# Two-layer decoder on one core: smaller groups in the quantised feed-forward, splits on other engines and in another order, and the last stage's base products started in the stage before

## The reference

```python
x = _layernorm(x + _L0_attn_ref(x, ...))       # a state-space mixer (hydra)
x = _layernorm(x + _L0_xattn_ref(x, ctx, ...)) # cross-attention, 16 heads of 96, 4 of k and v
x = _layernorm(x + _L0_ffn_ref(x, ...))        # quantised feed-forward, inner width 1792
x = _layernorm(x + _L1_attn_ref(x, ...))       # self-attention, 32 heads of 16, ALiBi
x = _layernorm(x + _L1_xattn_ref(x, ctx, ...)) # cross-attention, 32 heads of 128, 8 of k and v, rms norms
x = _layernorm(x + _L1_ffn_ref(x, ...))        # linear with routed LoRA

def _L0_ffn_ref(...):
    # dequantize(w, s, z) = (w - z) * s, with a row of z and s for every 128 rows of w
    gate = silu(x @ gate_proj)
    up = x @ up_proj
    return (gate * up) @ down_proj

def _L1_ffn_ref(...):
    q = x[:, 107:-1, :].mean(axis=1)
    routing = softmax(q @ router_W.T + router_b)
    base = x @ W.T + b
    t = einsum('bsd,erd->bser', x, A)
    return base + einsum('bser,eor,be->bso', t, B, routing) * 2
```

## Time and profile before

| | us |
|---|---|
| median of 3 runs | 1679.01 (1676.1 to 1681.4) |
| the profiled execution, its own time | 1680.96 |
| its span, first to last instruction | 1679.2 |
| PE busy | 1575.3 (94%) |
| DVE busy | 932.6 (56%) |
| ACT busy | 803.6 (48%) |
| POOL busy | 769.3 (46%) |
| mean granted clock of TensorE | 0.982 |

### The profile page before, as it was taken

The page is one execution under the profiler, slowest core; times in us unless marked ns, Lnnn a source line. Parts: engine busy times, 40 slices in busy tenths (PEclk is TensorE's granted clock), DMA queues, the critical chain, the costliest instruction groups (busy, mean ns, idle before and its releaser), DMA issues. The chain is left out here.

```text
span 1679.2 us, 29888 instructions
## 1 busy us (share of the span) xinstructions
PE 1575.3 (94%) x11188; PEld 1316.2 (78%) x11188; DVE 932.6 (56%) x1647; ACT 803.6 (48%) x2447; POOL 769.3 (46%) x625
## 2 busy tenths in 40 slices
PE   6999999999997699998999879999999999999978
PEld 3777897888886488878777678888888888888866
DVE  3847503333365778775667734555555555555755
ACT  3342325444443355536999724454454454544520
POOL 3403214343421788842533545555555545554423
PEclk9999999999999799999999999999999999999999
DMA  6100200010102552203000031101101101100001
GB/s 207 38 1 1 57 20 20 20 41 2 52 2 82 182 175 98 79 1 120 1 2 26 29 113 38 39 26 38 46 19 51 38 27 39 32 26 14 1 1 51
DMA packets 62258, 77.85 MB, mean 46 GB/s; under 512 B 12136, under 2 KB 41316, under 8 KB 62116
## 3 DMA queue, kind: packets, MB, share of 16 engines
q1 hardware_dynamic: 61652, 74.63, 13.9%
q0 software_dynamic: 464, 1.32, 0.3%
HBM read 73.85 MB, written 2.10 MB: 45 GB/s over the span
## 5 line engine op out<-in xcount | busy, mean ns | idle before, releaser
L1145 POOL TENSOR_TENSOR xa_rs<-xa_ms,minus_half 128x5 f32<-128x5 f32 x64 | 74.7, 1168 | 170.0 <-DVE xa_ms L1395 169.9
L1151 POOL TENSOR_TENSOR xa_prob<-xa_prob,xa_inv 128x512 f32<-128x512 f32 x64 | 66.7, 1042 | 136.2 <-DVE xa_inv L1362 136.2
L763 POOL TENSOR_TENSOR xa_prob<-xa_prob,xa_inv 128x1024 f32<-128x1024 f32 x32 | 60.7, 1896 | 140.8 <-DVE xa_inv L1023 140.8
L1342 ACT ACTIVATE xa_prob<-xa_prob,xa_peak 128x128 f32<-128x128 f32 x256 | 99.7, 391 | 41.9 <-DVE xa_peak L1406 41.9
L1390 DVE TENSOR_REDUCE xa_ssq<-pre 128x4 f32<-128x512 f32 x64 | 43.9, 686 | 135.6 <-ACT pre L1328 135.6
L1699 DVE SCALAR_TENSOR_TENSOR ff_acc<-ff_ring,ff_sT,ff_acc 128x512 f32<-128x512 f32 x140 | 100.4, 747 | 21.6 <-ACT ff_acc L1653 12.7
L1599 PE MATMUL ff_ring<-xT_hi,ff_w 128*128 128x512 f32 x224 | 91.7, 410 | 18.1 <-DVE ff_acc L1699 13.5
L100 PE MATMUL xa_qp<-late_q_hi,xT_hi 128*128 128x512 f32 x256 | 107.2, 419 | 0.0
L1328 ACT ACTIVATE pre<-xa_qp 128x512 f32<-128x512 f32 x64 | 38.2, 597 | 142.6 <-PE xa_qp L102 142.6
L100 PE MATMUL xa_rows<-late_o_hi,xa_out_hi 128*128 128x512 f32 x256 | 102.6, 401 | 1.9 <-DVE xtok L1369 1.9
L2092 ACT ACTIVATE pre<-pre,sa_peak 128x128 f32<-128x128 f32 x256 | 99.2, 397 | 9.5 <-DVE sa_peak L2131 9.3
(11 more groups left out here) (415 smaller groups left out, 5054.6 us busy)
## 6 DMA issues: line engine op xcount, KB each, us to landing
pre<-in_wq SPq DMA_DIRECT2D x8, 1024.0 KB, 5.8
late_raw_o<-in_wo SPq DMA_DIRECT2D x8, 1024.0 KB, 5.2
ff_dn_q<-in_down_w SPq DMA_DIRECT2D x7, 512.0 KB, 3.8
ff_dn_z<-in_down_z SPq DMA_DIRECT2D x7, 512.0 KB, 4.9
ff_dn_s<-in_down_s SPq DMA_DIRECT2D x7, 512.0 KB, 6.1
pre<-in_wq SPq DMA_DIRECT2D x16, 192.0 KB, 3.5
pre<-in_wo SPq DMA_DIRECT2D x16, 192.0 KB, 3.9
pre<-in_xT SPq DMA_DIRECT2D x2, 1024.0 KB, 13.7
```

The costliest lines, as they stand in the source:

```text
L763: pool.tensor_tensor(prob[:, t % 3, :, :], prob[:, t % 3, :, :], bc(inv[:, t % 3, :], 2, [P, Q, KEYS]), ALU.mult).then_inc(s["norm"], 1)
L1145: pool.tensor_tensor(rs[:, :], ms[:, :], m.minus_half[:, 0:Q + 1], ALU.pow).then_inc(s["rs"], 1)
L1151: pool.tensor_tensor(prob[:, u % 2, :, :], prob[:, u % 2, :, :], bc(inv[:, u % 2, :], 2, [P, Q, S]), ALU.mult).then_inc(s["norm"], 1)
L1342: last = act.activation(prob[:, u % 2, h, :], prob[:, u % 2, h, :], ACT.Exp, bias=peak[:, u % 2, h:h + 1], accum_out=total[:, u % 2, h:h + 1])
```

## The change

Six parts. (1) cross0's v weights are copied and subtracted in four pieces, PE waits for each in its first batch, and the fillers ahead go from 9 to 4. (2) ffn0's groups are made of one, two, two, one and one turns instead of two, two, two and one: rows are now 40 of 2 or 4 tiles. Rows, weights and down weights have new units; PE starts with the first piece of weights, fillers go from 7 to 2, and SP issues the gate and up loads of turn T + 1 ahead of `dn(T)`. (3) self's output weights are split on DVE. (4) cross1's first kv weights are split in two halves, with fewer fillers; in steps 0 to 7 POOL's splits have another order; the 20 fillers of step 2 are gone. (5) The banks of `qp`, `kvp`, `qt` and `score` are shared with lora, and `base(0)` to `base(3)` of lora are issued in cross1's tail, three in place of fillers. (6) lora begins with a low rank, has five row banks, and its last scale goes to ACT, for which DVE computes a shift. The core of the diff:

```diff
-                act.activation(v_hi, raw_v, ACT.Copy).then_inc(s["v_hi"], 1)
+                for c in range(KC):
+                    act.activation(v_hi[:, c, :], raw_v[:, c, :], ACT.Copy).then_inc(s["v_hi"], 1)
...
-                dve.wait_ge(s["v_hi"], 1)
-                dve.tensor_tensor(v_lo, raw_v, raw(v_hi), ALU.subtract).then_inc(s["v_lo"], 1)
+                for c in range(KC):
+                    dve.wait_ge(s["v_hi"], c + 1)
+                    dve.tensor_tensor(v_lo[:, c, :], raw_v[:, c, :], raw(v_hi[:, c, :]), ALU.subtract).then_inc(s["v_lo"], 1)
...
                     if t < 2:
                         roots(t)
-                        split_o(0, 2 * t)
-                        split_o(0, 2 * t + 1)
-                    if g <= G:
+                        split_o(0, t)
+                    if t == 2:
+                        split_o(0, 2)
+                        split_o(0, 3)
+                    if t == 3:
+                        split_kv(1, 0)
+                        split_kv(1, 1)
+                    if 4 <= t < B:
+                        split_q(1, b - 4)
+                        split_o(1, b - 4)
+                    if 1 < g <= G:
...
-                idle_products(pe, m, rows[:, 0:P], 5)
+                idle_products(pe, m, rows[:, 0:P], 2)
                 for t in range(UNITS):
                     project_kv(t)
                     if t == 2:
-                        idle_products(pe, m, rows[:, 0:P], 20)
+                        idle_products(pe, m, rows[:, 0:P], 0)
...
+                def base(b, read, n):
+                    pe.wait_ge(s["split_q"], PIECES_Q * G)
+                    pe.wait_ge(n4["lo"], b + 1)
+                    pe.wait_ge(s[read], n)
+                    for c in range(KC):
+                        three(pe, m.late.bank[b][:, :], m.xT_hi[:, c, b * P:(b + 1) * P], m.xT_lo[:, c, b * P:(b + 1) * P],
+                              q_hi[:, 0, c, :], q_lo[:, 0, c, :], c == 0, False)
+
                 scores(UNITS - 1)
+                base(0, "qn", UNITS)
                 out_rows(UNITS - 3)
                 turned(UNITS - 2)
                 turn_batch(UNITS - 4)
                 values(UNITS - 2)
-                idle_products(pe, m, qp[:, 0:P], 9)
+                pe.wait_ge(s["kn"], UNITS)
+                base(1, "v_lo", UNITS)
                 out_rows(UNITS - 2)
                 turned(UNITS - 1)
                 turn_batch(UNITS - 3)
                 values(UNITS - 1)
-                idle_products(pe, m, qp[:, 0:P], 6)
+                base(2, "qT", UNITS)
                 out_rows(UNITS - 1)
                 turn_batch(UNITS - 2)
-                idle_products(pe, m, qp[:, 0:P], 14)
+                base(3, "masked", UNITS)
                 turn_batch(UNITS - 1)
...
+GROUPS = ((0,), (1, 2), (3, 4), (5,), (6,))
+HALVES = 2 * len(GROUPS)
+TABLE = [(hb, k) for hb in range(HALVES) for k in range(MT * len(GROUPS[hb // 2]))]
...
+        mid = {3: [0, 1], 4: [2, 3], 5: [4, 5], 6: [6, 7], **{n: [n - 1] for n in range(9, 22)}, 22: [22], 23: [24, 25], 24: [26, 27],
+               25: [28, 29], 26: [30, 31], 27: [32, 33]}
+        end = {21: [21], 22: [23], 27: [34, 35]}
...
+        weight_units = {1: (1, 1, 2, 2), 2: (3, 4, 4, 5), 3: (6, 7, 8, 9), 4: (10, 11, 12, 13), 5: (14, 15, 16, 17), 6: (18, 19, 20, 21)}
+        down_units = {0: (1, 1, 1, 2, 2, 2), 1: (3, 3, 4, 5, 5, 6), 2: (7, 7, 7, 8, 8, 8), 3: (10, 10, 11, 12, 12, 13),
+                      4: (14, 14, 15, 16, 16, 16), 5: (18, 18, 19, 20, 20, 21), 6: (22, 22, 23, 24, 24, 25)}
...
                 for T in range(TURNS):
+                    if T < TURNS - 1:
+                        if T >= 2:
+                            sp.wait_ge(s["w"], KC * (T - 1))
+                        elif T == 1:
+                            sp.wait_ge(s["w_first"], KC)
+                        ffn_stage_inputs(sp, io, *stage[(T + 1) % 2], T + 1, s["ld_even" if T % 2 else "ld_odd"])
                     if T:
-                        if T >= 3:
-                            sp.wait_ge(s["w"], KC * (T - 2))
-                        elif T == 2:
-                            sp.wait_ge(s["w_first"], KC)
-                        ffn_stage_inputs(sp, io, *stage[T % 2], T, s["ld_odd" if T % 2 else "ld_even"])
                         sp.wait_ge(s["dn_sub"], T)
                         sp.wait_ge(s["dn_w"], MT * T)
...
-                pool.wait_ge(s["o_hi"], 1)
-                pool.tensor_tensor(wo_lo[:, :, :], raw_o, raw(wo_hi[:, :, :]), ALU.subtract).then_inc(s["o_lo"], 1)
...
+                dve.wait_ge(s["ld_o"], 16)
+                dve.tensor_copy(wo_hi[:, :, :], raw_o).then_inc(s["o_hi"], 1)
+                dve.wait_ge(s["o_hi"], 1)
+                dve.tensor_tensor(wo_lo[:, :, :], raw_o, raw(wo_hi[:, :, :]), ALU.subtract).then_inc(s["o_lo"], 1)
...
-                base(0)
+                low_rank(0)
...
+                low_rank(1)
                 pe.wait_ge(s["wide"], 1)
...
-                for b in range(1, B):
+                base(EARLY)
+                for b in range(EARLY):
+                    adapted(b)
+                for b in range(EARLY + 1, B):
+                    adapted(b - 1)
                     base(b)
-                    adapted(b - 1)
                 adapted(B - 1)
...
+                for b in range(B):
+                    act.wait_ge(s["shift"], b + 1)
+                    act.activation(m.xtok[:, b, :], m.xtok[:, b, :], ACT.Identity, bias=shift[:, b:b + 1],
+                                   scale=m.rstd[:, b:b + 1]).then_inc(n5["x"], 1)
...
+                def shifted(b):
+                    dve.wait_ge(n5["rstd"], b + 1)
+                    dve.tensor_scalar(shift[:, b:b + 1], m.meanvar[:, b, 0:1], m.rstd[:, b:b + 1], -1.0, ALU.mult, ALU.mult).then_inc(s["shift"], 1)
```

More of the change, by code:

```diff
@@ L55, with __init__ @@
 class Late:
-    def __init__(self, sb):
+    def __init__(self, sb, pb):
+        self.bank = [pb(f"late_bank{i}") for i in range(4)]
         self.q_hi, self.q_lo = (sb("late_" + n, [P, 2, KC, D], F32R) for n in ("q_hi", "q_lo"))
@@ L1061, in cross1_stage @@
         out_hi, out_lo = (sb(n, [P, 2, Q, S], F32R) for n in ("out_hi", "out_lo"))
-        qp, kvp, qt, kt, score, turn, mixed, rows = (pb(n) for n in ("qp", "kvp", "qt", "kt", "score", "turn", "mixed", "rows"))
+        qp, kvp, qt, score = m.late.bank
+        kt, turn, mixed, rows = (pb(n) for n in ("kt", "turn", "mixed", "rows"))
         s = {n: sem("xa1_" + n) for n in (
@@ L2179, in lora_stage @@
         low = [pb(f"low{i}") for i in range(2)]
-        rows = [pb(f"rows{i}") for i in range(BANKS)]
-        small, turned = pb("small"), pb("turned")
+        rows = [*m.late.bank, pb("rows4")]
+        small = pb("small")
+        turned = small[:, P:P + B]
+        shift = sb("shift", [P, B])
         s = {n: sem("lo_" + n) for n in (
-            "chain", "q", "logits", "lg", "exp", "wide", "wide_T", "route", "low", "t", "t_hi", "t_lo", "res", "rows", "add", "stored")}
+            "chain", "q", "logits", "lg", "exp", "wide", "wide_T", "route", "low", "t", "t_hi", "t_lo", "res", "rows", "add", "shift", "stored")}
         n5 = norm_sems(sem, "n5")
@@ L2256, in _ @@
                 dve.wait_ge(s["wide_T"], 1)
-                ch.step(dve.tensor_copy(route[:, :], turned[:, 0:B]))
+                ch.step(dve.tensor_copy(route[:, :], turned))
                 for n in range(2):
```

127 lines of the change are left out of this document (65 added, 62 removed).

## The result

The changed kernel takes 1654.97 us (median of 4 runs, 1651.71 to 1657.16), the kernel before 1677.78 beside it (4 runs, 1676.1 to 1681.4). The ratio is 0.986, with a 95% interval of 0.9835 to 0.9884: 19 to 28 us less. The profiled execution took 1657.16 with a span of 1654.0. The forecast was 30.5 us less, with 1649 for the median; both the range and the direction held, and the gain came out at three quarters to four fifths of what was worked out.

A forecast was written before the change was run, and what follows sets the result against it. PE was taken as the bound nearly everywhere, so gain comes only where it is not full: 2.3 + 9.5 + 0 + 9.2 + 9.5 = 30.5 off 1680.96 gives 1650.5, about 1649 for a median; range 1641 to 1661.

The forecast's parts named there:

- the 1.6 set aside for clock: ffn0: allowance of 1.6 us for the clock falling after PE's stalls, within the forecast gain of 9.5.
- step (c): ffn0: DVE ends unit 2, 5 × 0.747 and two weight pieces, at 555.4; first output row at about 557.3.
- step (e): ffn0: after unit 7, POOL's product, total, low and two down lows take some 7.0, putting row 8 at 598.2.
- rival B: ffn0's front: DVE and POOL hold it, nine pieces up to 0.55 longer each, row 8 at 603, time 1654; chance 0.16.
- the 7.6 of the sum: cross1's start: the turn of step 0's result comes at 1000.9 instead of 1008.54, 7.6 us of the forecast 9.2.
- the signs: cross1's start: normalisation of step 0 some 1 us behind its reciprocal, and the turn 9 us earlier.
- Rival C: cross1's tail: each moved `base` delays the chain it stands in, costing 11.2 instead of 3.3, time 1657; chance 0.07.
- Rival E: Feed-forward: `dn(T)`, issued behind stage T+1's loads, reaches DVE one unit late each turn, 39 us more, 1688; chance 0.03.
- (d): ffn0: units 3 to 6 take DVE 5.9 to 8.2 each, ending at 584.5, and unit 7 ends at 591.4.

The follow-up runs named there:

- the experiment on the order of loads: The changed kernel with SP's old order in the feed-forward, a turn's down weights ahead of the next turn's gate and up weights; ratio 0.9906 to the kernel before.

## Why the prediction was right, point by point

**cross0.** The first product at 171.96 (172.1 forecast). The gain of 2.3 is right as a mechanism and measured 2.15 in six kernels; the changed kernel's own profile shows 0.6, with 0.65 as the clock of its first 4 us. The clock was the item missing from this term: the prediction asked only whether PE was late, not at what clock it would start.

**ffn0.** Measured from the stage's first product: `down(0)` ended at +14.6 (+13.8 forecast), the first row stood at +24.4 (+23.2), row 8 at +66.8 (+64.1). Row 8 was mis-sized by 2.7, in two places, which the rows below show. The 2.7 lost at row 8 came back by half, since the 1.6 set aside for clock weren't needed in this profile. In others they were, and more: with the same feed-forward 223.2. Against a typical stage of before, 229.5 (three of four are 228.95 to 229.66), the gain lies between 6 and 10; ffn0 and self together took 443.1 to 445.5 in four kernels with the old feed-forward and 435.5 to 437.8 in five with the new one, 7.1 between the medians. The forecast of 9.5 was some 2 too high. From the changed kernel's timeline:

```profile
551.51 2.46 DVE L1756 TENSOR_TENSOR ff_w<-ff_other 128x512 fp32r<-128x512 int32 x2
...
590.90 2.51 POOL L1598 TENSOR_TENSOR ff_dn_w<-ff_dn_w,ff_dn_s 128x512 f32<-128x512 f32 x2
593.37 1.27 POOL L1585 TENSOR_TENSOR ff_acc<-ff_acc 128x512 f32<-128x512 f32 x1
```

The first place is the front. The load of `down(0)` landed at +13.4 where +12.5 was forecast, and the two pieces of weights of unit 2 took 2.46 where the sum had 2 × 0.757 = 1.51. So DVE ended unit 2 at about 556.2, +22.9 for the +21.3 of step (c), and unit 7 at about 592.1, +58.8 for +57.3: some 1.6 late at both, with nothing added in between. (In a unit DVE makes two parts, then the pieces, `down` and the row additions, then three parts; so of the five parts from 589.73 shown above, three are unit 7's.) The second place is step (e), which counts 7.0 of POOL's work from there, product, total, low and two down lows, and has no term for the two scales of `down(2)`. They hold POOL until 593.4, so the product starts 1.2 after DVE's end, and row 8 comes 8.0 behind it instead of 6.8.

The pieces are rival B's mechanism. Beside POOL's operations the eight pieces of units 2 to 7 took 9.3 instead of the 6.1 that 0.757 each would give. Its size, 4.5 less, was too large all the same: DVE needed 35.9 us from the end of unit 2 to that of unit 7 and was given 36.0, and its parts, most of its work, are not delayed.

**self.** Nothing from the splits, as forecast; the 1.9 us in the profile are clock, and 1.2 to 1.4 of them occur without the change.

**cross1's start.** Forecast 9.2, measured 9.0 between the two profiles. The turned probabilities came 7.6 earlier from the stage's first product, the 7.6 of the sum, though the signs had said 9; the rest is clock, as forecast. How near the two numbers are is partly luck, since the body of the same old code took 626.34 in one profile, which would leave 5.8 to 7.3. POOL's order alone is worth 8.2 to 9.5. The halves of the first weights and the fillers were not tested apart.

**Tail and lora.** Forecast +3.3, measured +3.26, and 3.2 to 3.3 in every kernel whose tail is the same. Rival C is dead. lora gave 12.5 (forecast 12.8) with 0.76 as the clock of its first 7 us, as in the kernel before, and 11.4 in profiles with 0.59 to 0.67 there. ACT's last scale takes 0.81, not 0.6.

**Rival E** stayed away, but the experiment on the order of loads shows that the queue it pointed to is the most sensitive part of the change: 8 to 12 us hang on it. The prediction priced the reordering of loads at nothing beyond turn 0, and its steps (c) and (d) hold no wait for the loads of turns 2 and 3, without saying what takes it away. That the term came out near is in this respect partly luck: with the old order the regrouped stage loses 2 to 3 us instead of gaining 9.5. It should have asked, for each turn, when SP may issue the load in either order.

**The sum.** 30.5 forecast. With typical lengths (cross1's body as in three of the four old profiles) it is 2.15 + 7.1 + 9.0 to 10.7 − 3.25 + 11.4 to 12.5 = 26.4 to 29.2, and by the medians 23 (beside each other) to 25 (1679.97 over 20 runs of the kernel before, less 1654.97). What remains between these is not settled: the first stage, which nothing touches, alone took 168.45 to 171.61 in these profiles, and a single execution of the changed kernel varies by 5.5.

## What to carry to other kernels

Where an engine works in order, ask what each instruction stands behind, in the new order and in the old: POOL's queue was worth 8 to 10 us and SP's 8 to 12, and neither shows as a busy engine. Where a row says that PE waits for DVE, look what DVE was waiting for. Work that is moved ahead fits a wait only up to the wait's length, so cut it to that size: four base products cost 3.3 us whole and 0.3 in quarters. And when stages differ by 1 or 2 us between two traces with the same idle rows, look at the granted clock before looking for a cause in the code.

## What the runs showed of the hardware

- The same wait of 2.56 or 2.57 us on PE was followed in three kernels by full clock and in two by some 5.6 us at half clock, with the same code around it. The price of such a wait is 2.6 or 5.4.
- DVE and POOL took turns also when DVE's operation was a copy of integers to fp32 with one input: 0.69 alone, 1.77 beside POOL.
- One run went at a mean clock of 0.32 and took 5454 us, while DVE's, ACT's and POOL's busy times stayed at 935, 813 and 758 us (944, 809 and 767 in the changed kernel). Only TensorE was slow. It happened once and was not reproduced.
